# Rotated rows of two heads kept one below the other, and scores as two products over 64 rows each

## The chip, the cores and the metric

One core of a Trainium2 chip runs the whole kernel. The metric is the device time of one execution in microseconds; lower is better. The engines are PE (TensorE, matrix products into PSUM banks), DVE (VectorE), ACT (ScalarE), POOL (GpSimd) and SP (which issues most of the DMAs). Each runs its own program in order, and semaphores hold them together.

## What is computed

A decoder layer on x of 16 sequences x 128 tokens x 256 features: layer norm, attention with 16 heads of 128 features, a second mixing block (a long convolution as triangular products), and a mixture of experts. Only the attention matters here:

```python
Q = jnp.einsum('btc,ncd->btnd', x, W_Q) + b_Q
K = jnp.einsum('btc,ncd->btnd', x, W_K) + b_K
V = jnp.einsum('btc,ncd->btnd', x, W_V) + b_V
Q = _apply_rope(Q, cos, sin)          # r1 = x1*cos - x2*sin ; r2 = x1*sin + x2*cos
K = _apply_rope(K, cos, sin)          # x1, x2: even and odd features of a head
scores = jnp.einsum('bqnd,bknd->bnqk', Q, K) / math.sqrt(d_head)
probs = jax.nn.softmax(jnp.where(causal[None, None], scores, -jnp.inf), axis=-1)
z = jnp.einsum('bnqk,bknd->bqnd', probs, V)
out = jnp.einsum('bqnd,ndm->bqm', z, W_O) + b_O
```

A score sums over the 128 rotated features of one head, 64 values r1 and 64 values r2.

## The kernel before

The attention runs in 4 groups of 4 sequences (GT = 512 tokens), and in each group over 8 pairs of heads. A group and a pair make a step, `s = 8 g + p`, 32 in all, and three more to empty the pipeline. The steps are pipelined by hand: while step s projects q and k of its pair, it also makes v and the scores of the pair before, transposes and weighs the probabilities of the pair before that, and applies the output projection to the pair before that. `live(k)` tells whether the k-th pair back exists. Every engine goes through the same steps with its own part, written out in `step` of each engine; the order inside a step is fixed by hand.

PE's step, in order: v of the last pair in two halves (24 records of L472 to L474, 128x256) into `v_bank`, which are banks 1 and 4; at p = 0 the transposes of xhat (L691); the output products (L705, 16 records); work of the next block placed beside (`beside_first`: transposes at p 0 to 3, convolution products L590 to L592 at p 4 to 7 of groups 1 to 3); for head 0 of the pair the transposes of its probabilities (L538, `transpose_probs`) and the scores (L731); for head 1 the transposes, then the value product of head 0 (L552, `weigh_values`) and the scores of head 1; the value product of head 1; `beside_second`; and the four projections of q and k, even and odd features (L472 to L474, 128x512), into banks 0, 1, 4 and 0. Bank 4, `pt_bank`, thus serves for v, for the transposes of probabilities, and for a projection. `transpose_probs(s, 0, ..)` waits for `v_taken` (ACT has copied v out of bank 4, L1038) and for `prob_ready[0]`, which POOL sets at L1180; head 1 waits for `pt_taken` (ACT's copy to prob_t, L1059) and `prob_ready[1]`, which DVE sets at L1389.

The columns of the weights are laid out so that one projection holds the 64 even features of head 0 in rows 0 to 63 and those of head 1 in rows 64 to 127 of a bank, and the next one the odd features likewise. DVE reads each bank once and writes two products, with cos and sin (L1369): `turn[m][0..3]` are even x cos, even x sin, odd x cos, odd x sin, for q (m = 0) and k (m = 1). The rotation then is t0 - t3 and t1 + t2. `rot[m][h]` holds the whole head h, r1 in rows 0 to 63 and r2 in rows 64 to 127. So the rotation takes eight operations of 64 rows a step: for each m, POOL makes r1 of head 0 (L1196) and r2 of head 1 (L1199), whose rows stay where they are, and DVE makes r1 of head 1 (L1382) and r2 of head 0 (L1385), which change halves.

DVE's step: the work beside, then for each head score x scale + mask (L1350) and its maximum (L1354), work beside again (`beside_scored`), the turns of q and of k with 1 / total behind each (L1358), the rotations, and prob[1] x 1 / total (L1389). POOL's step (`core_step`): the rotations of q, prob[0] x 1 / total (L1180), the rotations of k, then kv products of the next block (L1229) and, in groups 2 and 3 at p >= 4, four row scatters (L1207) and a wait for their landing. ACT copies v, prob_t and z_t out of PSUM and makes the exponentials (L1026); at p = 1 and 2 it also takes a square root for a layer norm, for which it waits for DVE.

Matrix products in f32 show as two records of PE each, with two weight loads (PEld); those of the f32r type as one.

Of the kernel before, what the change touches and what calls it, by code (L numbers as in the profile page):

```python
# [7 lines left out]
ALU = mybir.AluOpType  # L8
# [3 lines left out]
BATCH, SEQ, D = 16, 128, 256  # L12
HEADS, DH = 16, 128
PAIRS = HEADS // 2
GB = 4
GROUPS = BATCH // GB
GT = GB * SEQ
# [42 lines left out]
def decoder(nc, x_in, wqkv_in, bqk_in, bv_in, wo_in, bo_in, trig_in, mask_in, ident_in,  # L60
# [5 lines left out]
    with ExitStack() as ctx:  # L66
# [72 lines left out]
        rot = [[sb(f"rot{m}{h}", [128, GT], c=tctx) for h in range(2)] for m in range(2)]  # L139
# [325 lines left out]
        def _(pe):  # L465
# [202 lines left out]
            def step(g, p, live, first):  # L668
# [13 lines left out]
                if p == 0 and live(0):  # L682

                    pe.wait_ge(xhat_ready, g * GB + GB)
                    for c in range(CH):
# [7 lines left out]
                        last.then_inc(xt_ready, 1)  # L693
                if live(3):
# [20 lines left out]
                for h in range(2):  # L715
                    if live(2):
                        transpose_probs(s, h, live)
                        if h == 1:
                            weigh_values(s, p, 0, first)
                        if h == 1 and p == 3 and g > 0:  # L720
                            beside_first(g, p, live)
                    if live(1):

                        if h == 0:
                            pe.wait_ge(rot_dve, s * 4)
                            pe.wait_ge(rot_pool, s * 4)
                        if live(2):
                            pe.wait_ge(s_taken, s * 2 - 4 + h + 1)
                        for b in range(GB):
                            t = slice(b * SEQ, (b + 1) * SEQ)  # L730
                            last = nc.tensor.matmul(score[h][:, t], rot[0][h][:, t], rot[1][h][:, t],  # L731
                                                    start=True, stop=True)
                        last.then_inc(s_ready, 1)
                        if h == 0 and p == 0 and g > 0:
                            beside_first(g, p, live)
# [424 lines left out]
        def _(pool):  # L1160
# [32 lines left out]
            def pool_rot(m, s):  # L1193


                nc.gpsimd.tensor_tensor(rot[m][0][0:64, :], turn[m][0][0:64, :], turn[m][3][0:64, :],  # L1196
                                        ALU.subtract).then_inc(rot_pool, 1)
                pool.wait_ge(rot_pool, s * 4 + 2 * m + 1)
                nc.gpsimd.tensor_tensor(rot[m][1][64:128, :], turn[m][1][64:128, :], turn[m][2][64:128, :],  # L1199
                                        ALU.add).then_inc(rot_pool, 1)  # L1200
                pool.wait_ge(rot_pool, s * 4 + 2 * m + 2)
# [655 lines left out]
```

## Time and profile before

| | |
|---|---|
| median of 3 runs | 1054.18 us (1045.16 to 1055.42) |
| the profiled execution | 1055.78 us, span 1054.0 us |
| mean granted clock | 0.978 |
| PE busy | 974.7 us (92%) |
| PEld busy | 860.2 us (82%) |
| DVE busy | 834.7 us (79%) |
| POOL busy | 512.2 us (49%) |
| ACT busy | 379.1 us (36%) |

The attention stage lasts until about 700 us. A record of PE is modelled until its result is there, and the next can start well before, so what a product costs in a row of them is the distance from start to start, not its own duration. "Idle before <- releaser" in a row is the time in which the engine was empty before an instruction, and the instruction that ended it.

### The profile page before, as it was taken

To read this page: it belongs to the slowest core of one execution; us is meant where nothing else is said; L and a number is where in the kernel's file an instruction comes from. 1 tells how busy PE (TensorE), PEld (TensorE's weight loads), DVE (VectorE), ACT (ScalarE), POOL (GpSimd) and SP (SyncE) were. 2 spreads that over 40 slices of the span, in tenths; PEclk is the share of its full clock that TensorE was granted. 3 is DMA by queue.
4 is the path that set the end of the run, shared out by engine and by line. 5 is a ranking of instruction groups with operands and counts; after the bars stand their busy time and mean duration, and the time that the engine had idled before them with its cause. 6 is when DMAs were issued, how large, how long until landed. Compare 5 with 4: busy or idle time off the path is not lost.

```text
span 1054.0 us, 17503 instructions
## 1 busy us (share of the span) xinstructions
PE 974.7 (92%) x5621; PEld 860.2 (82%) x5621; DVE 834.7 (79%) x1596; ACT 379.1 (36%) x1077; POOL 512.2 (49%) x388
## 2 busy tenths in 40 slices
PE   3699999999999898999998999978999799999996
PEld 2588889889998887888887898866887699999984
DVE  4978998999889899988889998866576666666637
ACT  2245444352233443322344222252152244444420
POOL 1342544357633426576524558604614166666750
PEclk9899999999999999999989999999999899999999
DMA  8858958996446422102511220214141277777758
GB/s 287 311 210 339 351 212 333 407 392 240 170 145 232 156 83 81 60 32 91 201 61 61 81 82 21 104 59 184 52 191 61 59 118 120 122 118 119 122 81 296
DMA packets 68872, 169.83 MB, mean 161 GB/s; under 512 B 6704, under 2 KB 42416, under 8 KB 67760
## 3 DMA queue, kind: packets, MB, share of 16 engines
q1 hardware_dynamic: 54336, 149.66, 39.2%
q0 software_dynamic: 14448, 19.05, 11.0%
q8 instruction: 49, 0.80, 0.3%
q14 instruction: 39, 0.32, 0.1%
HBM read 82.69 MB, written 85.99 MB: 160 GB/s over the span
## 4 chain that ended last, share of the span: by engine, by line
PE 72%; DVE 19%; issue 4%; DMA 2%; ACT 2%; SPq 1%; DVEq 0%; POOLq 0%; ACTq 0%
PE bank L472 9%; PE bank L474 9%; PE bank L473 9%; PE bank L705 7%; PE bank L552 5%; PE bank L731 4%; DVE rot L1385 3%; PE bank L856 3%; PE bank L858 3%; PE bank L817 3%; DVE rot L1382 3%; PE bank L590 2%; PE bank L592 2%; PE bank L591 2%; PE bank L538 2%
## 5 line engine op out<-in xcount | busy, mean ns | idle before, releaser
L1196 POOL TENSOR_TENSOR rot<-turn 64x512 f32<-64x512 f32 x64 | 93.4, 1460 | 261.4 <-DVE turn L1369 239.4
L1369 DVE SCALAR_TENSOR_TENSOR turn<-bank,bqk,trig 128x1024 f32<-128x1024 f32 x128 | 160.9, 1276 | 17.9 <-PE bank L474 15.5
L1264 POOL DMA_INDIRECT sums<-ysb,token_at x79 | 123.1, 1558 | 78.1 <-DVE ysb L1737 35.4
L472 PE MATMUL bank<-xt_hi,w_hi 128*128 128x512 f32 x256 | 109.1, 426 | 14.0 <-DVE vcs L1418 5.0
L705 PE MATMUL bank<-wo,z_t 128*128 128x256 f32 x512 | 116.0, 379 | 0.8 <-ACT z_t L1064 0.8
L1229 POOL TENSOR_TENSOR kv<-c_t,v_t 128x512 f32<-128x512 f32 x64 | 69.3, 1098 | 97.3 <-ACT v_t L990 46.1
L705 PEld LDWEIGHTS bank<-wo,z_t 128*128 128x128 f32 x512 | 94.9, 190 | 12.8 <-ACT z_t L1064 1.0
L1026 ACT ACTIVATE prob<-prob,negmax 128x128 f32<-128x128 f32 x256 | 99.2, 391 | 9.3 <-DVE negmax L1354 9.3
L474 PE MATMUL bank<-xt_hi,w_lo 128*128 128x512 f32 x256 | 102.1, 399 | 0.0
L473 PE MATMUL bank<-xt_lo,w_hi 128*128 128x512 f32 x256 | 102.0, 398 | 0.0
L1038 ACT COPY v<-bank 128x512 f32<-128x512 f32 x64 | 37.5, 587 | 165.6 <-PE bank L474 165.6
L1385 DVE TENSOR_TENSOR rot<-turn 64x512 f32<-64x512 f32 x64 | 95.0, 1485 | 2.0
L1199 POOL TENSOR_TENSOR rot<-turn 64x512 f32<-64x512 f32 x64 | 92.4, 1444 | 5.0
L1207 POOL DMA_INDIRECT xs<-xh,dest x64 | 63.3, 989 | 51.3 <-DVE dest L1521 33.4
L1059 ACT COPY prob_t<-bank 128x512 f32<-128x512 f32 x64 | 37.6, 588 | 135.8 <-PE bank L538 135.8
L731 PE MATMUL bank<-rot 128*128 128x128 f32 x512 | 71.5, 285 | 8.8 <-DVE rot L1385 5.4
L1382 DVE TENSOR_TENSOR rot<-turn 64x512 f32<-64x512 f32 x64 | 77.8, 1216 | 2.0
L552 PE MATMUL bank<-prob_t,v 128*128 128x128 f32 x512 | 72.4, 286 | 5.5 <-DVE logit L1463 2.4
L1730 DVE TENSOR_TENSOR eh<-bank,eh 128x176 f32<-128x176 f32 x79 | 27.0, 342 | 61.7 <-ACT eh L1138 61.7
L731 PEld LDWEIGHTS bank<-rot 128*128 128x128 f32 x512 | 65.2, 200 | 10.8 <-DVE rot L1385 6.5
L472 PEld LDWEIGHTS bank<-xt_hi,w_hi 128*128 128x128 f32 x256 | 49.9, 195 | 28.3 <-DVE turn L1369 5.8
L472 PE MATMUL bank<-w_hi,xt_hi 128*128 128x256 f32 x256 | 72.6, 284 | 0.0
(194 smaller groups left out, 2468.3 us busy)
## 6 DMA issues: line engine op xcount, KB each, us to landing
xs<-zeros SPq DMA_DIRECT2D x12, 3710.0 KB, 16.9
w_hi<-w_dram SPq DMA_DIRECT2D x24, 768.0 KB, 4.2
w_lo<-w_dram SPq DMA_DIRECT2D x24, 768.0 KB, 7.0
xe_all<-xs SPq DMA_DIRECT2D x79, 132.5 KB
sums<-zeros SPq DMA_DIRECT2D x3, 2176.0 KB, 12.6
raw<-in_wqkv SPq DMA_DIRECT2D x16, 384.0 KB, 4.3
w_dram<-w_hi SPq DMA_DIRECT2D x8, 768.0 KB, 6.0
w_dram<-w_lo SPq DMA_DIRECT2D x8, 768.0 KB, 7.4
```

The lines of the kernel that those rows point to most:

```text
L472: nc.tensor.matmul(o, lh, rh, start=(i == 0), stop=False)
L473: nc.tensor.matmul(o, lh, rl, start=False, stop=False)
L474: last = nc.tensor.matmul(o, ll, rh, start=False, stop=(i == n - 1))
L552: last = nc.tensor.matmul(zt_bank[:, b * 128:(b + 1) * 128], v[p % 2][:, b, h * DH:(h + 1) * DH], prob_t[h][:, b, :], start=True, stop=True)
L705: last = nc.tensor.matmul(acc[b // 2][:, (b % 2) * D:(b % 2 + 1) * D], z_t[h][:, b, :], wo[:, 2 * r + h, :], start=(r == 0 and b % 2 == 0 ...
L731: last = nc.tensor.matmul(score[h][:, t], rot[0][h][:, t], rot[1][h][:, t], start=True, stop=True)
L1026: last = nc.scalar.activation(prob[h][:, b, :], prob[h][:, b, :], ACT.Exp, bias=negmax[:, h, b:b + 1], accum_out=total[:, h, b:b + 1])
L1196: nc.gpsimd.tensor_tensor(rot[m][0][0:64, :], turn[m][0][0:64, :], turn[m][3][0:64, :], ALU.subtract).then_inc(rot_pool, 1)
L1264: nc.gpsimd.indirect_dma_start(sums_dram[s % YBUFS], bass.IndirectOffsetOnAxis(ap=token_at[:, s:s + 1], axis=0), ysb[s % YBUFS][:], None, ...
L1369: last = nc.vector.scalar_tensor_tensor(turn_all[m][:, 2 * i:2 * i + 2, :], qk_bank[2 * m + i][:].unsqueeze(1).to_broadcast([128, 2, GT]), ...
L1382: nc.vector.tensor_tensor(rot[m][1][0:64, :], t[0][64:128, :], t[3][64:128, :], ALU.subtract).then_inc(rot_dve, 1)
L1385: nc.vector.tensor_tensor(rot[m][0][64:128, :], t[1][0:64, :], t[2][0:64, :], ALU.add).then_inc(rot_dve, 1)
```

## The change

`rot[m][0]` now holds r1 of both heads, head 0 in rows 0 to 63 and head 1 in rows 64 to 127, and `rot[m][1]` holds r2 of both in the same way. DVE makes `rot[m][0]` and POOL `rot[m][1]`, each in one operation over 128 rows for q and one for k. A score then is the sum of two products over 64 rows, r1 with r1 and r2 with r2, accumulated in PSUM; those of head 0 use rows 0 to 63 and those of head 1 rows 64 to 127. Both heads' scores stand together in PE's order, behind the transposes of head 1 and the value product of head 0, and the transposes of head 0 stand ahead of the output products. The counts that the semaphores are waited for change with it.

```diff
@@ PE's step, behind the transposes of xhat
+                if live(2):
+                    transpose_probs(s, 0, live)
                 if live(3):
...
@@ PE's step, behind the output products and beside_first
-                for h in range(2):
+                if live(2):
+                    transpose_probs(s, 1, live)
+                    weigh_values(s, p, 0, first)
+                    if p == 3 and g > 0:
+                        beside_first(g, p, live)
+                if live(1):
+                    pe.wait_ge(rot_dve, s * 2)
+                    pe.wait_ge(rot_pool, s * 2)
                     if live(2):
-                        transpose_probs(s, h, live)
-                        if h == 1:
-                            weigh_values(s, p, 0, first)
-                        if h == 1 and p == 3 and g > 0:
-                            beside_first(g, p, live)
-                    if live(1):
-
-                        if h == 0:
-                            pe.wait_ge(rot_dve, s * 4)
-                            pe.wait_ge(rot_pool, s * 4)
-                        if live(2):
-                            pe.wait_ge(s_taken, s * 2 - 4 + h + 1)
-                        for b in range(GB):
-                            t = slice(b * SEQ, (b + 1) * SEQ)
-                            last = nc.tensor.matmul(score[h][:, t], rot[0][h][:, t], rot[1][h][:, t],
-                                                    start=True, stop=True)
-                        last.then_inc(s_ready, 1)
-                        if h == 0 and p == 0 and g > 0:
-                            beside_first(g, p, live)
+                        pe.wait_ge(s_taken, s * 2 - 2)
+                    for b in range(GB):
+                        t = slice(b * SEQ, (b + 1) * SEQ)
+                        for i in range(2):
+                            for h in range(2):
+                                rows = slice(64 * h, 64 * h + 64)
+                                last = nc.tensor.matmul(score[h][:, t], rot[0][i][rows, t], rot[1][i][rows, t],
+                                                        start=(i == 0), stop=(i == 1))
+                                if b == GB - 1 and i == 1:
+                                    last.then_inc(s_ready, 1)
+                    if p == 0 and g > 0:
+                        beside_first(g, p, live)
...
@@ POOL
-                nc.gpsimd.tensor_tensor(rot[m][0][0:64, :], turn[m][0][0:64, :], turn[m][3][0:64, :],
-                                        ALU.subtract).then_inc(rot_pool, 1)
-                pool.wait_ge(rot_pool, s * 4 + 2 * m + 1)
-                nc.gpsimd.tensor_tensor(rot[m][1][64:128, :], turn[m][1][64:128, :], turn[m][2][64:128, :],
-                                        ALU.add).then_inc(rot_pool, 1)
-                pool.wait_ge(rot_pool, s * 4 + 2 * m + 2)
+                nc.gpsimd.tensor_tensor(rot[m][1][:], turn[m][1], turn[m][2], ALU.add).then_inc(rot_pool, 1)
+                pool.wait_ge(rot_pool, s * 2 + m + 1)
...
@@ DVE
-                        nc.vector.tensor_tensor(rot[m][1][0:64, :], t[0][64:128, :], t[3][64:128, :],
-                                                ALU.subtract).then_inc(rot_dve, 1)
-                    if live(0):
-                        nc.vector.tensor_tensor(rot[m][0][64:128, :], t[1][0:64, :], t[2][0:64, :],
-                                                ALU.add).then_inc(rot_dve, 1)
+                        nc.vector.tensor_tensor(rot[m][0][:], t[0], t[3], ALU.subtract).then_inc(rot_dve, 1)
```

## Rows read from the trace of the kernel before

**Rows 1.** The page: busy tenths in 40 slices of the span, 26.35 us each
```profile
PE   3699999999999898999998999978999799999996
DVE  4978998999889899988889998866576666666637
```

**Rows 2.** Stretches of the attention: start and end, us; PE, PEld, DVE, ACT, POOL busy; PEclk; DMA
```profile
60.00:215.00 155.00, 152.89 (x945) 134.88 (x944) 136.43 (x162) 74.59 (x223) 62.20 (x42) 1.00 0.85 326
215.00:340.00 125.00, 123.55 (x748) 110.72 (x747) 114.01 (x138) 43.18 (x138) 66.34 (x50) 1.00 0.63 227
350.00:520.00 170.00, 160.81 (x966) 143.33 (x967) 152.39 (x224) 61.42 (x190) 93.92 (x74) 0.98 0.22 82
520.00:700.00 180.00, 165.92 (x997) 147.74 (x996) 153.74 (x245) 65.60 (x197) 92.97 (x73) 0.97 0.20 72
```

**Rows 3.** The chain of waits, 440 to 500 us: start, length, what
```profile
461.85 0.86 issue
...
465.17 0.89 PE bank L731 x8
466.06 1.00 PE bank L552 x8
...
488.68 1.00 PE bank L552 x8
```

**Rows 4.** What PE waited for: us in total, times, longest us
```profile
PE bank L538 <- ACT prob_t L1059: 8.7, 4, 3.0
PE bank L731 <- DVE rot L1385: 5.4, 5, 4.1
PE bank L472 <- DVE vcs L1418: 5.0, 2, 2.5
PE bank L731 <- issue: 3.4, 4, 0.9
PE bank L552 <- DVE logit L1463: 2.4, 2, 1.2
PE bank L552 <- DVE pos L1515: 2.3, 2, 1.2
```

**Rows 5.** One line each: count, duration ns min/median/max, first and last start
```profile
L1382 DVE TENSOR_TENSOR rot<-turn x64: 686/1601/1672, 30.4 to 678.9; 64x512 f32<-64x512 f32 x64
...
L1772 DVE TENSOR_TENSOR x<-x,ys x24: 680/691/694, 1030.1 to 1049.1; 128x512 f32<-128x512 f32 x24
```

**Rows 6.** Timeline of DVE at 30 to 36 us, first and last of four rotations
```profile
30.43 0.94 DVE L1382 TENSOR_TENSOR rot<-turn 64x512 f32<-64x512 f32 x1
...
34.74 0.68 DVE L1385 TENSOR_TENSOR rot<-turn 64x512 f32<-64x512 f32 x1
```

**Rows 7.** Line L731: count of records, duration ns min/median/max
```profile
L731 PE MATMUL bank<-rot x512: 275/275/426, 35.5 to 686.2; 128*128 128x128 f32 x171
```

**Rows 8.** The stretch behind the wait for vcs, columns as in rows 2
```profile
400.50:404.50 4.00, 3.18 (x8) 2.55 (x9) 2.77 (x5) 2.18 (x13) 0.00 (x0) 0.57 0.37 101
```

**Rows 9.** Timeline of PE and ACT at 61 to 63 us, step 2
```profile
61.30 0.28 PE L474 MATMUL bank<-w_hi,xt_lo 128*128 128x256 f32 x1
62.34 0.63 PE L538 MATMUL bank<-ident,prob 128*128 128x128 f32 x4 [0.77 <-ACT v L1038]
...
61.61 0.59 ACT L1038 COPY v<-bank 128x512 f32<-128x512 f32 x1 [0.85 <-PE bank L474]
```

**Rows 10.** Timeline of PE and POOL at 454 to 460 us, group 2, p = 6
```profile
455.08 0.28 PE L474 MATMUL bank<-w_hi,xt_lo 128*128 128x256 f32 x1
...
456.54 1.60 POOL L1199 TENSOR_TENSOR rot<-turn 64x512 f32<-64x512 f32 x1
458.22 1.37 POOL L1180 TENSOR_TENSOR prob<-prob,rtotal 128x512 f32<-128x512 f32 x1
```

**Rows 11.** Timeline of PE at 380 us: products of 18 columns
```profile
380.02 0.26 PE L521 MATMUL bank<-gate_hi,th_early 128*128 128x18 f32 x1
380.13 0.26 PE L522 MATMUL bank<-gate_lo,th_early 128*128 128x18 f32 x1
```

More of the change, by code:

```diff
@@ L138, in decoder @@
         turn = [[t[:, i, :] for i in range(4)] for t in turn_all]
-        rot = [[sb(f"rot{m}{h}", [128, GT], c=tctx) for h in range(2)] for m in range(2)]
+        rot = [[sb(f"rot{m}{i}", [128, GT], c=tctx) for i in range(2)] for m in range(2)]
         v = [sb(f"v{i}", [128, GB, 2 * DH], c=tctx) for i in range(2)]
@@ L1366, in step @@
                             if i == 0 and live(1):
-                                dve.wait_ge(rot_pool, s * 4 - 2 + 2 * m)
-                                dve.wait_ge(rot_dve, s * 4 - 2 + 2 * m)
+                                dve.wait_ge(rot_pool, s * 2 - 1 + m)
+                                dve.wait_ge(rot_dve, s * 2 - 1 + m)
                             last = nc.vector.scalar_tensor_tensor(
```

## The prediction

> **What bounds the kernel now.** I read the slices of the span first. In the attention stage (about 60 to 700 us) PE shows 9 in nearly every slice and DVE 8 and 9 [rows 1]. So two engines are nearly full, and the next question is which of them is waited for. The stretches answer it: from 60 to 340 us PE is busy 276 of 280 us, from 350 to 700 us 327 of 350 us, while DVE has 250 of 280 and 306 of 350, and the granted clock is 1.00 in the first two stretches and 0.98 and 0.97 in the others [rows 2]. PE sets the pace, and DVE is close enough behind to stop it now and then.
>
> The chain of waits shows the same in time: in group 2 the last value products of one step start at 466.06 and of the next at 488.68 us, 22.6 us apart, and what lies between is PE work one piece after the other; the one wait in such a step is of 0.86 us [rows 3]. A step of PE work that is added there is added to the time, and one that is taken off DVE is worth only the PE waits that DVE causes.
>
> Those are in the list of waits. The reader is to see how small it is: PE bank L731, the scores, waits 5.4 us on DVE's rotation in all, 4.1 of it at the very first step, and 3.4 us ("issue") on POOL's; L538 8.7 us on ACT's prob_t copy, L472 5.0 us on vcs, L552 2.4 and 2.3 us on logit and pos [rows 4]. All but the first lie in the steps in which DVE carries routing work as well, at the start of groups 2 and 3, or where POOL is late.
>
> **Part 1: the rotation on DVE and POOL.** Before, each does four operations over 64 rows a step, after, two over 128 rows. A row more costs nothing on these engines: 128x512 from SBUF takes 0.691 us on DVE (L1772) against a minimum of 0.686 for 64x512 (L1382) [rows 5]. The common 1.6 us of the rotations is what they take while POOL works too. So DVE loses two operations of 1.2 to 1.6 us a step, some 3 us with the gaps, POOL two of about the same. Over 32 steps that is about 90 us off each engine, none of it directly off the end. What it gives back are PE waits:
>
> - POOL's last rotation ended late in four steps (p = 6 and 7 of groups 2 and 3), so the scores waited 0.86 us, 3.4 in all [rows 4]. A wait costs some 0.16 us more than it shows, because a product's record lasts 0.275 us where the next can start after 0.11 (8 records of L731 in 0.89 us) [rows 3, 4, 7]. 4 x 1.02 = 4.1 us.
> - DVE's lateness at the start of groups 2 and 3: the two longest of L538, 5.9 of its 8.7 us (behind ACT, which waits for DVE's moments of the tokens), 5.0 (vcs), 2.4 (logit), 2.3 (pos) = 15.6 us, with 8 x 0.16 for the pipeline 17 us [rows 4]. Four rotations in a row take DVE some 5 us (30.43 to 35.42 in the first step, [rows 6]), and those four stand ahead of the moments and of the turns that are late here; two fewer take away about 3 us. Behind the wait for vcs the granted clock is at its lower level, 0.57 of full on average from 400.5 to 404.5 us [rows 8]. The clock of 0.98 over 170 us and of 0.97 over 180 us [rows 2] is 8.8 us lost; the tail's waits keep a part, I take 5. Together 22 us.
> - The first step: the scores start at 35.48, after rotations from 30.43 to 35.42 [rows 6]. Two of them are left, one of 0.9 us as the first, and one of 1.6 us as is common beside POOL: 2.4 us earlier. The other short waits of L731 on DVE: 5.4 - 4.1 = 1.3 us.
>
> In sum 4.1 + 22 + 2.4 + 1.3 = 30 us off. The ends: 15 if DVE's lateness stays by half, and 45 if every slack of PE in the stage went.
>
> **Part 2: the transposes of head 0 are moved ahead of the output products L705.** transpose_probs(0) writes pt_bank, which has just been v_bank[1]: it waits until ACT has copied v (v_taken), and now it stands right behind the product of v. Before, 16 records of L705 (3.46 us) stood between. The trace has this very order once, in step 2, where L705 isn't live yet: last v product starts 61.30, ACT's copy 61.61 for 0.59 us, L538 at 62.34, so 1.04 us from start to start instead of the 0.12 of a record [rows 9]. The wait costs 0.92 us. It comes in every step with live(1) and live(2), 31 steps, but for the three p = 0 in which the xhat transposes lie between (16 records of L691, about 1.7 us), and step 2 has it already: 27 x 0.92 = 24.8 us. Queued behind it on PE is everything: L705, the turns beside, scores, the next projections. Nothing covers it, since PE is the bound.
>
> The same move also asks for prob[0] some 3.5 to 6 us earlier. It is POOL's multiplication L1180. In most steps it is done: POOL's rotation before it is shorter by one operation. In four it isn't: at step p = 6 of group 2 POOL comes late out of its row scatters, rotates until 458.14, and L1180 ends at 459.59 [rows 10]. Without L1199, 1.68 us from start to start, it ends at 457.9. The transposes could start at 455.08 + 1.04 = 456.1 [rows 9, 10]. Price 1.8 us, in p = 6 and 7 of groups 2 and 3 (the steps of [rows 4]'s four "issue" waits): 7.2 us. The copies of prob_t on ACT then lie beside L705, and the second transposes find theirs done; no gain, as before the score product of 0.9 us hid it.
>
> **Part 3: both heads' scores stand together, behind transposes 1 and value product 0.** DVE gets head 0 about 3 us later, and has both prob and negmax (four operations of 128x512, 0.69 us each as L1772 in [rows 5]) behind the end of the scores. In a step with convolutions PE has then 0.9 (L552) + 2.6 (12 convolution records) + 4.1 us (three projections) before the fourth, which needs the first turn. DVE: 0.2 + 2.75, the second conv's product is ready at 3.7, 0.7, two sums 1.3, turn 1.28, so 7.0 against 7.6. Hidden, with 0.6 us left; if that is gone it costs 12 steps a few tenths, up to 4 us.
>
> **Part 4: the score products.** Before 16 records a step: 4 batches, 2 heads, 2 records for an f32 product, 0.112 us apart (8 in 0.89 us, [rows 3]). After there are 16 products over 64 rows, 32 records. Does the row count make one cheaper? The stream is 128 columns either way, and the trace has no product over 64 rows. From below: the halves work side by side, two records in the time of one, and 32 records take the 1.8 us of 16: nothing is added. From above: they come one behind the other. The row that is nearest is that of the gate: 18 columns instead of 512, and still 0.111 us from start to start, one weight load each [rows 11]. Weights of 128 columns come no faster than one in 0.11 us when they follow each other on one array. That is 16 more records x 0.112 = 1.79 us a step, 57 us in 32 steps. Should nothing overlap, 1024 records of 0.275 us would be 282 - 57 = 225 us more.
>
> Which? Heads alternate in the loop and their results lie in different banks (2 and 3), so nothing orders one half behind the other but the queue. A pair shares no row, no bank and no weight cell. I take the lower end, with a chance little above even, because the weight load, not the stream, is the neck at 128 columns, and only if loads too run side by side is the second half free.
>
> The Trainium skill (TensorEngine Tiling (Array Packing), "Key Properties") says that different tiles can execute weight loads and products in parallel; no row here shows it, and by it the sum gets nothing from part 4. The same list says that changing the tiling mode drains the engine, which speaks against the change: by it each step pays two drains.
>
> A drain I bound by the rows: from nothing to what a record lasts beyond the next start, 0.275 - 0.112 = 0.163 us [rows 3, 7]. Two changes a step, 64 in all: 0 to 10.4 us, I take the middle, 5.2.
>
> **Sum.** -30 + 24.8 + 7.2 + 0 + 5.2 = +7 us on the profiled execution's own 1055.8 us (span 1054.0 and 1.8 around it), 1063. The three runs' median is 1054.18, 1.6 lower, so against them 1061.
>
> **Rivals.** (A) is the forecast: halves side by side, the relief of DVE eaten by the two waits of the moved transposes. Its own range is 1046 to 1078: the gain between 15 and 45, drains from 0 to 10, part 3 up to 4, not all at their ends together. Chance 0.50.
>
> (B) The halves' weight loads take turns. Place: the scores, every step. Price 57 us, 1055.8 + 7 + 57 = 1120, or 1118 against the median. For it speaks the gate's row, where loads set the pace; against it that loads there go to the same rows. It decides as soon as the second half adds more than 0.3 us a step (10 us). Chance 0.28.
>
> (C) They overlap by part, two records in 1.5 times one: +28 us, 1091. Chance 0.12.
>
> (D) Faster: DVE and POOL also set PE's small slacks between 60 and 340 us and in the last steps, all of the 45 us comes back, with no drain, and the wait on v is half hidden where PE would have waited for DVE. 1055.8 - 45 + 12 + 7 = 1030; with half of that 1043. For it: the 90 us off DVE; against it the exact period of rows 3. Chance 0.08.
>
> (E) No pipelining between halves at all, +100 us and more. 0.02.
>
> **How the numbers follow.** What a measurement of this kernel can tell from no change is about 1%, 10.5 us. Of A six parts in ten are within 1%, three over it, one below: 0.05 faster, 0.30 same, 0.15 slower. B, C and E are slower (0.42), D is faster (0.08). Faster 0.13, same 0.30, slower 0.57. The likeliest case gives 1061; the range must take in B, so it goes from 1046 to 1120 and leaves out D's better half and E.
>
> **What would show it.** L538 waiting on ACT v some 27 times for about 0.77 us, and four times on POOL's prob: part 2. DVE and POOL busy 90 us less each, rotations 128x512 x64 on each engine: part 1. The score records: 1024 instead of 512; if pairs start together, 32 records in 1.8 us, A; in 3.6 us, B. A gap of 0.1 to 0.2 us before the first score and before the value product behind them is the drain. No more waits of L472 on vcs or L552 on pos. I am wrong if PE doesn't wait for v's copy, if DVE's lateness in groups 2 and 3 is still there, or if half-height records cost something that no row shows.

## The result, and the profile after

The changed kernel takes 1083.23 us, median of four runs (1079.05 to 1087.37), against 1054.46 of four runs of before beside it (1045.16 to 1055.42). The ratio is 1.031 (95% interval 1.027 to 1.034), so it is slower by 29 us. The profiled execution took 1086.12 us with a span of 1084.3 us and a mean granted clock of 0.973, so 30.3 us more span than before. The attention stage, up to the first product of the gate, ends at 739.2 us where before it ended at 706.6, 32.6 us later; the rest is 2.3 us shorter. So the whole of it lies in the attention.

The page: busy time by engine, and PE, DVE and granted clock in 40 slices, 27.1 us each; [rows 1] has the same of before.

```profile
PE 988.1 (91%) x6133; PEld 864.4 (80%) x6133; DVE 721.6 (67%) x1532; ACT 378.7 (35%) x1077; POOL 407.4 (38%) x324
...
PE   3789889899999989999989998979899899999996
...
DVE  4856656677766887666768875635676566666647
...
PEclk9899999999999999999999999988999899999998
```

DVE is busy 113 us less than before and POOL 105 us less, so DVE's slices of 8 and 9 are 5 to 8 now. And still PE, which was a 9 nearly everywhere, has 8s: it stands still more often, though nothing beside it is fuller. The stretches, columns as in [rows 2]:

```profile
60.00:215.00 155.00, 141.87 (x984) 122.22 (x983) 100.38 (x126) 66.35 (x200) 34.38 (x25) 1.00 0.79 302
215.00:340.00 125.00, 121.17 (x808) 106.91 (x807) 91.34 (x129) 41.72 (x134) 45.05 (x36) 1.00 0.60 216
350.00:520.00 170.00, 158.86 (x1036) 139.83 (x1037) 123.80 (x215) 58.79 (x184) 63.73 (x54) 0.97 0.28 101
520.00:700.00 180.00, 168.59 (x1123) 148.66 (x1122) 125.74 (x217) 62.62 (x191) 69.67 (x59) 0.97 0.21 77
```

From 60 to 340 us PE is empty 17 of 280 us, before 3.6. What it is empty for is in the list of waits (us in total, times, longest us), which answers to [rows 4]:

```profile
PE bank L538 <- ACT v L1040: 18.4, 24, 0.8
PE bank L538 <- ACT prob_t L1061: 15.8, 11, 2.8
...
PE bank L538 <- POOL prob L1182: 14.2, 5, 4.5
...
PE bank L732 <- DVE rot L1380: 1.3, 1, 1.3
```

All three large ones stand at L538, the transposes of probabilities. L472's waits on vcs, L552's on logit and pos, and four of the five on DVE's rotation, which before's list had, are gone.

### The profile page after: what moved, and what is told of

It reads as the page before. It is cut to its first block, busy times and chain, and to the rows that moved or that the text cites. A ratio compares the mean times of both kernels' runs of the same rounds, so it can differ in the third digit from the quotient of the medians.

```text
span 1084.3 us, 18399 instructions
## 1 busy us (share of the span) xinstructions
PE 988.1 (91%) x6133; PEld 864.4 (80%) x6133; DVE 721.6 (67%) x1532; ACT 378.7 (35%) x1077; POOL 407.4 (38%) x324
## 4 chain that ended last, share of the span: by engine, by line
PE 81%; DVE 6%; issue 4%; ACT 3%; POOL 2%; DMA 2%; SPq 1%; POOLq 0%; DVEq 0%; ACTq 0%
PE bank L707 11%; PE bank L472 9%; PE bank L474 9%; PE bank L473 9%; PE bank L552 6%; PE bank L732 6%; PE bank L538 3%; PE bank L858 3%; PE bank L860 3%; PE bank L819 3%; PE bank L590 2%; PE bank L592 2%; PE bank L591 2%; PE bank L521 2%; PE bank L522 2%
## 5 line engine op out<-in xcount | busy, mean ns | idle before, releaser
L1198 POOL TENSOR_TENSOR rot<-turn 128x512 f32<-128x512 f32 x64 | 93.3, 1457 | 340.4 <-DVE rtotal L1356 282.9
L707 PE MATMUL bank<-wo,z_t 128*128 128x256 f32 x512 | 124.3, 399 | 0.0
L472 PE MATMUL bank<-xt_hi,w_hi 128*128 128x512 f32 x256 | 108.0, 422 | 8.3 <-DVE w_lo L1321 3.2
L707 PEld LDWEIGHTS bank<-wo,z_t 128*128 128x128 f32 x512 | 101.0, 203 | 14.1
L1348 DVE SCALAR_TENSOR_TENSOR prob<-bank,mask 128x512 f32<-128x512 f32 x64 | 43.8, 684 | 86.4 <-PE bank L732 86.4
L1422 DVE TENSOR_TENSOR zc<-bank,c_t 128x512 f32<-128x512 f32 x64 | 44.0, 687 | 79.8 <-PE bank L592 79.6
L538 PE MATMUL bank<-ident,prob 128*128 128x128 f32 x256 | 40.7, 283 | 48.4 <-ACT v L1040 18.4
L538 PEld LDWEIGHTS bank<-ident,prob 128*128 128x128 f32 x256 | 29.1, 143 | 60.7 <-issue 43.2
L472 PE MATMUL bank<-w_hi,xt_hi 128*128 128x256 f32 x256 | 73.8, 288 | 0.0
L473 PE MATMUL bank<-w_lo,xt_hi 128*128 128x256 f32 x256 | 73.8, 288 | 0.0
L474 PE MATMUL bank<-w_hi,xt_lo 128*128 128x256 f32 x256 | 73.7, 288 | 0.0
L552 PE MATMUL bank<-prob_t,v 128*128 128x128 f32 x512 | 71.6, 283 | 0.8 <-ACT z_t L1066 0.8
L1380 DVE TENSOR_TENSOR rot<-turn 128x512 f32<-128x512 f32 x64 | 71.0, 1150 | 0.0
```

What stands on the lines that cost most here:

```text
L472: nc.tensor.matmul(o, lh, rh, start=(i == 0), stop=False)
L473: nc.tensor.matmul(o, lh, rl, start=False, stop=False)
L474: last = nc.tensor.matmul(o, ll, rh, start=False, stop=(i == n - 1))
L538: last = nc.tensor.transpose(pt_bank[:, b * 128:(b + 1) * 128], prob[h][:, b, :], ident[:])
L552: last = nc.tensor.matmul(zt_bank[:, b * 128:(b + 1) * 128], v[p % 2][:, b, h * DH:(h + 1) * DH], prob_t[h][:, b, :], start=True, stop=True)
L707: last = nc.tensor.matmul(acc[b // 2][:, (b % 2) * D:(b % 2 + 1) * D], z_t[h][:, b, :], wo[:, 2 * r + h, :], start=(r == 0 and b % 2 == 0 ...
```

## Experiments

Theory 1 is the prediction's, made exact on the trace of after: the halves work side by side, DVE's relief is worth about 30 us, and the loss comes from where the transposes stand (waits on v, on POOL's prob and, which the prediction had not, on prob_t), with some 10 us for the changes of tiling. Theory 2, the main rival, puts the loss into the half-height products themselves, whatever stands beside them. Changed and before run on several chips here, and before alone differs between them (1043.6, 1049.7 and 1051.3 us), so each number below is taken against before or another kernel on the same chip, or as a ratio to it. Three kernels (the rotation alone, and two with whole-height scores) compute other scores than the reference; that other numbers leave the time alone was not tried by itself, but all kernels with whole-height scores run the same number of PE records as before (5621).

### The transposes moved, nothing else

Before's rotation and scores are kept; only `transpose_probs(s, 0, live)` goes ahead of the output products.

```diff
@@ before, PE's step
+                if live(2):
+                    transpose_probs(s, 0, live)
                 if live(3):
...
                 for h in range(2):
                     if live(2):
-                        transpose_probs(s, h, live)
+                        if h == 1:
+                            transpose_probs(s, 1, live)
```

> The kernel before with one edit: the transposes of head 0 stand ahead of the output products, as in the changed kernel; rotation and scores as before. Theory 1 (the loss comes from where the transposes stand): 27 waits of 0.92 us on the copy of v, 25 us; four waits on POOL's prob of about 3.5 us instead of 1.6, as POOL still rotates twice, 14 us, less the 4 us that the scores waited there; about 11 waits of 1.4 us on the copy of prob_t behind ACT's other copies, 16 us; some of it lies in DVE's lateness, -10: about 1095, from 1085 to 1108. Theory 2 (the half-height products are the loss, the place is neutral): within 6 us of before, 1048 to 1060.

Measured: 1084.11 us against 1043.55, ratio 1.038 (1.033 to 1.043), so +41 us. The 1095 expected was meant against a kernel before of 1054 us, so it was +41 us too. Its waits of PE:

```profile
PE bank L538 <- POOL prob L1182: 20.7, 5, 4.3
PE bank L538 <- ACT v L1040: 18.4, 24, 0.8
...
PE bank L538 <- ACT prob_t L1061: 10.1, 11, 2.8
PE bank L472 <- DVE vcs L1420: 5.0, 2, 2.5
```

The 24 waits on v are there to the tenth, with no half-height product in the kernel. The move by itself is worth more than the whole loss of the change. POOL's waits are longer than in the changed kernel (20.7 against 14.2 us), since POOL still has its four rotations a step, and the wait on vcs is back, since DVE has.

### The rotation alone

The rotation of 128 rows, with before's order and one product over 128 rows for a score, which then is not the reference's.

```diff
@@ the changed kernel, PE's step: before's order and
-                                last = nc.tensor.matmul(score[h][:, t], rot[0][i][rows, t], rot[1][i][rows, t],
-                                                        start=(i == 0), stop=(i == 1))
+                            last = nc.tensor.matmul(score[h][:, t], rot[0][h][:, t], rot[1][h][:, t],
+                                                    start=True, stop=True)
```

> The changed kernel's rotation alone: one operation over 128 rows each for DVE and POOL, but PE in the order of before and with whole-height products as before. The scores therefore sum r1 of both heads with r1 and r2 with r2, which is not what the reference computes; only the time is of use. Theory 1: the relief of DVE and POOL is worth 30 us, 1024, from 1015 to 1035. Theory 2 says nothing against it. Theory 3 (the relief is off the path and was worth nothing): 1050 to 1057.

Measured: 1010.53 against 1043.55 us, ratio 0.967 (0.963 to 0.971): 33 us less, 30 expected. Its stretches, columns as above:

```profile
60.00:215.00 155.00, 154.16 (x956) 136.90 (x957) 115.73 (x150) 74.70 (x224) 38.41 (x28) 1.00 0.87 334
...
350.00:520.00 170.00, 170.00 (x1053) 153.21 (x1052) 135.26 (x225) 65.82 (x204) 74.35 (x62) 1.00 0.26 96
```

PE is busy 170.0 of 170 us at a granted clock of 1.00 from 350 to 520 us. That is what the relief of DVE and POOL gives when PE's order is left alone: no slack is left in this stretch.

### The halves one after the other

Half-height products in before's order: all of head 0, then, behind the transposes of head 1, all of head 1. A half never stands beside the other.

```diff
@@ on the kernel of the experiment before
                         for b in range(GB):
                             t = slice(b * SEQ, (b + 1) * SEQ)
+                            rows = slice(64 * h, 64 * h + 64)
+                            for i in range(2):
-                            last = nc.tensor.matmul(score[h][:, t], rot[0][h][:, t], rot[1][h][:, t], ...
+                                last = nc.tensor.matmul(score[h][:, t], rot[0][i][rows, t], rot[1][i][rows, t], ...
```

> The changed kernel's rotation and half-height products, but PE in the order of before: the scores of head 0 behind its transposes, those of head 1 behind the value product of head 0, so that the halves never stand side by side. Theory 1: 1024 + 16 more records a step that now come one behind the other at 0.11 us, 57 us, + two more changes of tiling a step at 0.1 us, and the first two, 13 us: 1094, from 1080 to 1105. Theory 2: a half-height product is slow whatever stands beside it; then the time is that of the changed kernel less its 25 us on v, about 1058. A third, that 64 rows load and stream in half the time: 1030 to 1040.

Measured: 1081.71 us, 71 more than the rotation alone; 70 expected. Timeline of PE: start, length, what. First this kernel at 283 us, then the changed one at 456 us:

```profile
282.80 0.60 PE L538 MATMUL bank<-ident,prob 128*128 128x128 f32 x4
283.33 2.05 PE L733 MATMUL bank<-rot 64*128 64x128 f32 x16
285.31 0.66 PE L538 MATMUL bank<-ident,prob 128*128 128x128 f32 x4
```

```profile
454.88 0.60 PE L538 MATMUL bank<-ident,prob 128*128 128x128 f32 x4
455.32 1.06 PE L552 MATMUL bank<-prob_t,v 128*128 128x128 f32 x8
456.31 2.06 PE L732 MATMUL bank<-rot 64*128 64x128 f32 x32
458.29 1.16 PE L552 MATMUL bank<-prob_t,v 128*128 128x128 f32 x8
```

Sixteen records of one half take 1.98 us from start to the next start, and 32 records of both halves in turn take 1.98 us too. Inside such a block the records of one half follow each other at 0.112 us, weight loads and products alike, as whole-height ones do. In the changed kernel they come in pairs 0.006 us apart, weight loads as well as products, and the pairs 0.112 us apart. So the second half is free, loads included, but only if the heads alternate. Theory 2, by which a half-height product costs the same whatever stands beside it, expected about 1058 us here; it falls. What is left of it is a price for each block, which the next kernel shows and the last two measure.

### The changed kernel with whole-height scores

The order of the changed kernel; each score is one product over 128 rows of `rot[.][h]`, and again not the reference's.

```diff
-                        for i in range(2):
-                            for h in range(2):
-                                rows = slice(64 * h, 64 * h + 64)
-                                last = nc.tensor.matmul(score[h][:, t], rot[0][i][rows, t], rot[1][i][rows, t],
-                                                        start=(i == 0), stop=(i == 1))
+                        for h in range(2):
+                            last = nc.tensor.matmul(score[h][:, t], rot[0][h][:, t], rot[1][h][:, t],
+                                                    start=True, stop=True)
```

> The changed kernel with its order, but whole-height score products over both heads' rows, 16 records a step instead of 32, no change of tiling; the scores are not the reference's, only the time is of use. Theory 1: the two gaps of 0.1 us a step and the 0.12 us that the 32 records take more go, 0.22 x 32 = 7 us less than the changed kernel, 1076, from 1070 to 1080. Theory 2 (the half-height products are the loss): 25 to 35 us less, 1048 to 1058.

Measured: 1060.83 against 1043.55 us, ratio 1.015 (1.011 to 1.020). The changed kernel's 1.031 is 16 us above it, where 7 was expected. So the half-height products do cost something, more than the prediction's 5.2 us, and this was the reason for a closer look at the tiling below. Not all of the 16 us is theirs: by the account described below, the lower level of the granted clock costs about 12 us in this kernel and 16 in the changed one, which leaves some 12 us for the products.

### The beside work ahead of the transposes of head 0

`beside_first` is moved from behind the output products to ahead of the transposes of head 0. It then stands between the product of v and the transposes, where PE waited for the copy of v; and the transposes of head 1 no longer stand right behind work whose copy ACT must make first.

```diff
+                if g == 0 or p not in (0, 3):
+                    beside_first(g, p, live)
                 if live(2):
                     transpose_probs(s, 0, live)
...
-                if g == 0 or p not in (0, 3):
-                    beside_first(g, p, live)
```

> The changed kernel with one edit in PE's order: the work beside (beside_first, where it stands ahead of the transposes of head 1) is moved from behind the output products to the front of the transposes of head 0. So it covers the copy of v, and the output products cover ACT's copies of that work and of prob_t. Theory 1 (three waits behind the moved transposes make the loss): about 21 of the 27 waits on v go, 19 us, the four on POOL's prob of 1.6 us, 6 us, and ten of the eleven on the copy of prob_t, 15 us, and some half-speed clock behind the longer ones, 3 us: 43 us less than the changed kernel, so some 11 us less than the kernel before, ratio 0.989, from 0.980 to 0.997. Rival: the work beside needs all four turns of DVE and POOL's kv products 3.5 us earlier, and the waits only move there: ratio 1.01 to 1.02.

Measured: 1046.05 us, against 1049.69 of before (ratio 0.996, 0.993 to 0.998) and 1084.85 of the changed kernel, which ran again on this chip (ratio 1.031, 1.028 to 1.034).

> The changed kernel as it is, on the chip of these runs, so that differences can be taken on one chip. Both theories: ratio 1.03 to the kernel before.

That is 39 us off by a change of place alone; 43 was expected. What is left of the waits:

```profile
PE bank L538 <- ACT prob_t L1061: 6.1, 4, 2.8
PE bank L538 <- ACT v L1040: 5.4, 7, 0.8
PE bank L538 <- POOL prob L1182: 4.7, 2, 4.5
```

### ACT's copy of prob_t[0] put first

ACT makes the copy of prob_t[0] ahead of its own work beside, not behind it. PE's order is that of the changed kernel.

```diff
@@ ACT's step, behind the copies of xt_hi
+                if live(2):
+                    act.wait_ge(pt_ready, s * 2 - 4 + 1)
+                    if live(3):
+                        act.wait_ge(zt_ready, s * 2 - 6 + 1)
+                    nc.scalar.copy(prob_t[0][:], ...).then_inc(pt_taken, 1)
...
-                    for i in range(4):
+                    for i in range(1, 4):
```

> The changed kernel with one edit in ACT's order: the copy of prob_t of head 0 comes right behind the copies of v and of xhat, ahead of the square root and of the copies of toep, c_t and tokens. Theory 1: the eleven waits of the second transposes on that copy (15.8 us of idle, 17 from start to start) go, while the copies that now come 0.6 us later are waited for by nobody for longer than before: 13 to 18 us less than the changed kernel, ratio to before 1.013 to 1.019. Rival: the second transposes would wait anyway, for the bank's own turn or for prob of head 1, and the time is that of the changed kernel, ratio 1.03.

Measured: 1069.74 us, 15 us less than the changed kernel beside it, in the 13 to 18 expected. The place is seen in the changed kernel at 93 to 100 us, PE and then ACT; what is in brackets is the idle time before and what ended it:

```profile
92.95 0.63 PE L538 MATMUL bank<-ident,prob 128*128 128x128 f32 x4 [0.77 <-ACT v L1040]
93.42 3.62 PE L707 MATMUL bank<-wo,z_t 128*128 128x256 f32 x16
96.87 1.88 PE L561 MATMUL bank<-toep,turned 128*128 128x512 f32 x4
100.01 0.63 PE L538 MATMUL bank<-ident,prob 128*128 128x128 f32 x4 [1.26 <-ACT prob_t L1061]
```

```profile
97.93 0.58 ACT L986 COPY toep<-bank 128x512 f32<-128x512 f32 x1 [3.66 <-PE bank L561]
98.79 0.58 ACT L986 COPY toep<-bank 128x512 f32<-128x512 f32 x1 [0.27 <-PE bank L561]
99.27 0.59 ACT L1061 COPY prob_t<-bank 128x512 f32<-128x512 f32 x1
```

PE finished transposing head 0 at 93.6 us. ACT stood empty for 3.66 us until 97.93, with the copy of prob_t[0] third in its queue behind two copies of convolution matrices (L986), which PE had not made yet; it made them right before the transposes of head 1. The engine was free, the data were there, and the order of the queue kept them apart. With ACT's copy first, the wait on prob_t is all but gone:

```profile
PE bank L538 <- POOL prob L1187: 14.4, 5, 4.5
...
PE bank L538 <- ACT prob_t L1050: 0.8, 1, 0.8
```

### The transposes late where POOL or ACT are late

This is built on the kernel with the beside work ahead. At p = 3 of groups 1 to 3 no beside work stood ahead of head 0's transposes, and in the second emptying step not even v does. There, and in the first emptying step, head 0's transposes stand behind the output products again, as before. At p = 3 and in the first emptying step the beside work lies between the two transposes.

```diff
+                late = g > 0 and (p == 3 or (p == 0 and g == GROUPS))
-                if live(2):
+                if live(2) and live(1) and not late:
                     transpose_probs(s, 0, live)
...
@@ behind the output products
                 if live(2):
+                    if late or not live(1):
+                        transpose_probs(s, 0, live)
+                    if late:
+                        beside_first(g, p, live)
                     transpose_probs(s, 1, live)
                     weigh_values(s, p, 0, first)
-                    if p == 3 and g > 0:
-                        beside_first(g, p, live)
...
@@ behind the scores
-                    if p == 0 and g > 0:
+                    if p == 0 and 0 < g < GROUPS:
                         beside_first(g, p, live)
```

> As with the work beside ahead of the transposes of head 0, and besides: in the steps p = 3 of groups 1 to 3 and in the first emptying step the transposes of head 0 stand behind the output products and the work beside stands between them and the transposes of head 1; in the second emptying step, too, they stand behind the output products. Theory 1: four more waits on v of 0.92 us go, and 2 of the 4.7 us that PE waits for POOL in the second emptying step: 5 to 6 us less than without, ratio to before about 0.984. Rival: at p = 3 the work beside then waits for DVE's normalised tokens, which it needs 1.3 us earlier: no difference.

Measured: 1032.95 against 1049.69 us, ratio 0.984 (0.981 to 0.986), and 13 us less than the version it is built on; only 5 to 6 were expected. By the account described below, waits behind the product of v fall from 6.6 us to 2.8, and 3.8 go at the second emptying step (4.7 us on POOL's prob, then 0.8 on z_t in its place). The expectation left out the granted clock, whose lower level costs 10.2 us in the version with the beside work ahead and 5.7 here. This kernel is faster than the kernel before and the changed one, and ran again on a third chip at 1032.51 against 1051.26 us (0.984, 0.981 to 0.987):

> The kernel of e8 again, on the chip of these runs, for the differences. Both: ratio to before 0.984.

### The tiling's price measured from both sides

A block is a run of half-height products between whole-height ones. In one kernel the number of blocks is doubled (two batches of the scores ahead of the value product of head 0, two behind), and in another they are taken away (whole-height scores, so not the reference's). Both are made on the last kernel, in which few waits are left that could hide a price, and run beside it.

```diff
@@ two blocks a step
+                    score_part(range(0, 2))
+                if live(2):
+                    weigh_values(s, p, 0, first)
+                if live(1):
+                    score_part(range(2, GB))
```

> As e8 (the fastest so far), but the scores in two parts of two batches each, one ahead of and one behind the value product of head 0: as many half-height records as in e8, twice as many changes between whole and half height. Theory 1 (a block of half-height products costs by its two changes): the stalls around a block, 0.15 at its first products, 0.09 ahead of it, 0.15 + 0.1 behind it, are paid once more in 32 steps, 0.45 us each: 10 to 15 us more than e8, ratio to before about 0.996. Rival (the stalls belong to the first use of fresh rotated rows, or the records themselves are dearer, not the change): within 3 us of e8, 0.984 to 0.987.

> As e8, but whole-height score products, 16 records a step, over both heads' rows; the scores are not the reference's, only the time is of use. Theory 1: all that the half-height products cost goes, about 11 us while the clock is full: ratio to before about 0.973. Rival (the 17 us between e4 and the changed kernel were waits that the order brings): less than 4 us, 0.980 to 0.984.

Measured: two blocks 1044.81 us, one block 1032.51, none 1021.22. That is +12.3 and -11.3 us for 32 blocks, so 0.35 us for a block one way and 0.38 the other. PE with no block (whole height), with one and with two:

```profile
240.90 1.06 PE L552 MATMUL bank<-prob_t,v 128*128 128x128 f32 x8
241.79 1.95 PE L733 MATMUL bank<-rot 128*128 128x128 f32 x16
243.58 1.06 PE L552 MATMUL bank<-prob_t,v 128*128 128x128 f32 x8
244.47 0.38 PE L590 MATMUL bank<-kv,toep 128*128 128x256 f32 x1
```

```profile
244.00 1.06 PE L552 MATMUL bank<-prob_t,v 128*128 128x128 f32 x8
244.99 2.06 PE L735 MATMUL bank<-rot 64*128 64x128 f32 x32
246.97 1.16 PE L552 MATMUL bank<-prob_t,v 128*128 128x128 f32 x8
247.97 0.60 PE L590 MATMUL bank<-kv,toep 128*128 128x256 f32 x2
```

```profile
248.13 1.16 PE L730 MATMUL bank<-rot 64*128 64x128 f32 x16
249.22 1.16 PE L552 MATMUL bank<-prob_t,v 128*128 128x128 f32 x8
250.31 1.16 PE L730 MATMUL bank<-rot 64*128 64x128 f32 x16
```

Whole height: the three groups take 0.89 + 1.79 + 0.89 = 3.57 us from start to start. With the block: 0.99 + 1.98 + 1.00 = 3.97. So the product ahead of the block is 0.10 us longer, the one behind it 0.11, and the block itself 0.19, though its pairs follow each other at the 0.112 us of whole-height records. The loss sits in two steps from start to start at each change of height, which the changed kernel shows at 456 us (the last value product, the first pair of the block, its second pair and the one behind it):

```profile
456.10 0.28 PE L552 MATMUL bank<-prob_t,v 128*128 128x128 f32 x1
456.31 0.38 PE L732 MATMUL bank<-rot 64*128 64x128 f32 x2
456.52 0.39 PE L732 MATMUL bank<-rot 64*128 64x128 f32 x4
```

The step across the change is 0.205 us and the next one, from the first pair to the second, 0.213, where both are 0.112 elsewhere. Behind the block the value product has the same two. That is 0.09 + 0.10 us for a change and 0.39 for the two of a block. In the last of these kernels the value product between two blocks takes 1.09 us, 0.20 more than its 0.89: it pays on both sides.

## Why the prediction was right and wrong

It said 1061 (1046 to 1120), with 0.57 for slower. The measured 1083 lies in the range, on the side that had most of the chance, but 5 us above the likeliest case's own range of 1046 to 1078. The range reached as far as 1083 only to take in rival (B), and of the 0.57 for slower 0.42 belonged to rivals in which the two halves don't run fully side by side. The runs rule these out, so range and direction held in part by luck. The likeliest case named the places rightly but for one: halves side by side, DVE relieved, PE waiting for v and for POOL. Its sum was 22 us short, by a wait that it put at nothing and by prices that it took too low.

The account below is made from start to start of PE's records up to the first gate product, each interval against the median of its kind in before. Between the rotation alone and the changed kernel stand 69.3 us of stage (669.9 and 739.2 us), and 36.7 between before and the rotation alone (the profile of the latter is of another chip: the two spans differ by 44.2 us where the medians on one chip differ by 33, and 7.5 of them lie behind the stage, so 3 to 4 us of the 36.7 are loose).

| term of the sum | forecast | measured |
|---|---|---|
| relief by the rotation | -30 | -36.7 in the stage; -33 in the medians |
| wait on the copy of v | +24.8 (27 x 0.92) | 25.1 (27 x 0.93) |
| wait on POOL's prob, four steps | +7.2 (4 x 1.8) | 6.6 beyond the wait on v |
| second half of the scores | 0 | 0; pairs at 0.112 us |
| changes of tiling | +5.2 (64 x 0.08) | 11 to 12 (32 x 0.35 to 0.38) |
| wait of the second transposes on prob_t | 0 | 17.6 in eleven, against one of 2.5 in the rotation alone |
| second emptying step, wait on POOL's prob | 0 | 4.7, before 1.0 on z_t at its place |
| lower level of the clock | inside the relief | 16.2 in all, before 9.6, rotation alone 1.6 |

From the rotation alone to the changed kernel: 25.1 + 6.6 + 15.1 + 4.7 + 11 + 14.6 = 77 us, and 7 us come off at other waits, which are shorter because PE asks later (3.4 at the projections, 1.8 at the gate, 1.7 in the emptying steps). That leaves 70 against the 69.3 measured. From before it is -36.7 + 69.3 = 32.6 us.

**Part 1 was right**, place and size. Rotations over 128 rows take DVE 0.681 us in the median where the 64 rows of L1382 took 1.601 [rows 5]:

```profile
L1380 DVE TENSOR_TENSOR rot<-turn x64: 659/681/1781, 30.6 to 702.3; 128x512 f32<-128x512 f32 x64
```

So the cost of rows was read rightly. The median hides two kinds: 36 of the 64 take 0.66 to 0.69 us and 28 take 1.76 to 1.78. Most of both lie beside a rotation of POOL, and what parts them is which began first. In all 28 long ones an operation of POOL with two inputs was running as DVE's began, in the short ones but for one it began later or not at all. DVE, then POOL, at 272 us:

```profile
271.91 0.66 DVE L1380 TENSOR_TENSOR rot<-turn 128x512 f32<-128x512 f32 x1
272.49 1.78 DVE L1380 TENSOR_TENSOR rot<-turn 128x512 f32<-128x512 f32 x1
```

```profile
272.04 1.68 POOL L1198 TENSOR_TENSOR rot<-turn 128x512 f32<-128x512 f32 x1
```

So the prediction's "1.6 us is what they take while POOL works too" holds only for those that begin second. DVE's busy time fell by 113 us, not by 90, and POOL's by 105.

**Part 2 was right in what it named.** Of the 28 waits behind the product of v, 24 are 0.93 us from start to start (one of them was there before), and in the other four POOL is the later one. Group 2, p = 6, PE and then POOL:

```profile
472.73 1.11 PE L538 MATMUL bank<-ident,prob 128*128 128x128 f32 x4 [2.34 <-POOL prob L1182]
```

```profile
469.93 1.30 POOL L1198 TENSOR_TENSOR rot<-turn 128x512 f32<-128x512 f32 x1 [1.56 <-DMA xs<-xh,dest]
471.30 1.37 POOL L1182 TENSOR_TENSOR prob<-prob,rtotal 128x512 f32<-128x512 f32 x1
```

The row scatters hold POOL, then come one rotation and the multiplication, and then PE: the chain of [rows 10], one rotation shorter.

**The step that failed** is the sentence behind it: "the copies of prob_t on ACT then lie beside L705, and the second transposes find theirs done". ACT has time enough (35% busy), but the sentence leaves out what is queued ahead of the copy. The term was put at 0 and measured 15.1 us more than in the rotation alone. Before, PE's beside work stood ahead of the transposes of head 0, and so ahead of the copy in both queues. Moving the transposes past it on PE turned the order round on PE alone; ACT still wanted the beside results first. Moving the copy on ACT shows it by itself (15 us), and with the work moved on PE the eleven waits are four.

**The change of tiling was mis-sized.** The bound by what a record lasts beyond the next start, 0 to 10.4 us for all, ended below the truth, and the middle was half of it. It counted one stall at each change, where there are two, 0.09 us in the step across it and 0.10 in the next. The Trainium skill (TensorEngine Tiling (Array Packing), "Key Properties") says that changing the tiling mode drains the engine; the trace agrees, with 0.205 us across a change where other records follow at 0.112. The Trainium skill says in the same section that different tiles can load weights and multiply in parallel. The trace agrees here too: two weight loads start 0.006 us apart in the changed kernel, and 0.11 us apart when the heads stand apart.

**The clock** was put in as a gain of 5 us, and not asked again for the new waits. The lower level comes back with them. Behind the wait for POOL above:

```profile
472.50:476.00 3.50, 3.27 (x10) 2.83 (x11) 0.00 (x0) 0.58 (x1) 3.34 (x3) 0.51 0.01 2
```

The granted clock (third figure from the end) is 0.51 there, the lower of the two levels. It is so behind each of POOL's four waits of 2.3 to 2.6 us and behind the 4.5 and 2.8 us of the second emptying step. Twice more, at 401 and at 582 us, it falls with no wait in the 13 us ahead; PE was busy in all 12.9 us from 388 to 400.9. The first of the two:

```profile
401.00:405.00 4.00, 3.46 (x17) 3.21 (x16) 3.83 (x11) 1.09 (x2) 0.00 (x0) 0.59 0.00 0
```

Why it falls there stays open. The rotation alone lost only 1.6 us to the lower level in the stage, the changed kernel 16.2.

**Part 3 was right**: DVE now waits 86.4 us for the scores in all (15.7 before), and PE's projections wait for DVE's turns only ahead of 50 us, 2.8 us in all against 4.1 before.

Of its signs of being wrong one came true in part: that half-height records cost something that no row shows. That is the second stall of each change.

What stays open: both heads' transposes stand ahead of the scores, because DVE writes prob[0] and prob[1] anew once the scores are there. Scores ahead of the transposes of head 1 would need another buffer, and weren't tried. Nor was it asked why the second step at a change of height costs 0.10 us more.

## What to carry to other kernels

When an instruction is moved on one engine, write down for each engine that answers it what stands ahead of the answer in its queue: an engine idle for 65% of the span kept PE waiting for 1.4 us on average, eleven times. A transpose or product that reuses a bank just filled waits for the engine that empties it, here 0.93 us each time, so put there the work that needs nothing: with this, and the transposes late where nothing stood ahead of them, the same change turned from 3.1% slower to 1.6% faster. The second half of half-height products is free only if the halves alternate; halves apart cost as much as whole products. Keep them in one block, as each block costs 0.35 to 0.38 us.

## What the runs showed of the hardware

- Weight loads of the upper and lower half ran beside each other: loads 0.006 us apart in f32, with 128 columns, so 32 records took 1.98 us where 16 of one half took the same.
- Each change between whole-height and half-height products cost 0.09 us in the step across it and 0.10 us in the next step, 11 to 12 us in 32 blocks, measured by adding as many (+12.3 us) and by taking them away (-11.3 us).
- A two-input operation of DVE on 128x512 f32 took 0.66 to 0.69 us when it began ahead of POOL's and 1.76 to 1.78 us when it began while POOL's was running (28 of 64).
- A bank that PE fills, ACT copies (0.59 us for 128x512 f32) and PE fills again cost 0.93 us of PE's time.
- Behind the wait of PE that ended at 472.73 us (2.34 us) the granted clock was 0.51; between 60 and 215 us, with waits of 0.8 to 1.4 us, it stayed at 1.00; at 401 us it fell although PE had been busy for all of the 12.9 us ahead. The lower level cost 16.2 us in the stage, 6.6 more than before.
